# Gate and up side by side in weight chunks, 256-column low-rank products, a turned front, and variance sums, banks and copies moved

## The reference

```python
def _dequant(codes, scales):              # blocks of 64
    w = NF4[codes]
    return (w.reshape(O, I // 64, 64) * scales[:, :, None]).reshape(O, I)
def _lin_lora(x, W, A, B):
    return x @ W.T + (x @ A.T) @ B.T      # A: 16 x I, B: O x 16
q, k, v = (_lin_lora(x, W[i], A[i], B[i]) for i in range(3))
x1 = x + _lin_lora((q + k + v) / 3, Wo, Ao, Bo)
h  = silu(_lin_lora(x1, Wg, Ag, Bg)) * _lin_lora(x1, Wu, Au, Bu)     # 1792 wide
x  = layernorm(x + x1 + _lin_lora(h, Wd, Ad, Bd))
x  = layernorm(x + _lin_lora(x, Wf, Af, Bf))   # NF4, rank 64, factor 1/4
x  = layernorm(x + attention(x))               # one head of 128 per batch
x  = layernorm(x + experts(x))                 # 64 experts of rank 16, best 16
```

## Time and profile before

| what | us |
| --- | --- |
| time, median of 3 runs (lowest, highest) | 526.01 (523.20, 526.26) |
| the profiled execution | 525.68 |
| its span in the trace | 523.9 |
| TensorE busy | 486.5 |
| VectorE, ScalarE, GpSimd busy | 374.4, 291.4, 284.2 |

### The profile page before, as it was taken

One profiled execution on the slowest core, in us unless ns is written; L12 is line 12 of the kernel. 1 busy time (PEld: TensorE's weight loads), 2 busy tenths in 40 slices (PEclk: granted clock), 3 DMA queues, 4 the chain that ended last, 5 costly groups with the idle time before them and its releaser, 6 DMA issues.

```text
span 523.9 us, 7456 instructions
## 1 busy us (share of the span) xinstructions
PE 486.5 (93%) x2248; PEld 393.9 (75%) x2248; DVE 374.4 (71%) x701; ACT 291.4 (56%) x539; POOL 284.2 (54%) x261
## 2 busy tenths in 40 slices
PE   2489899899999999999999998998998899999996
PEld 1246678688888888888888886887886788888884
DVE  5979889638897887997979953864368866366433
ACT  6979868555755675766666722625487422333021
POOL 4787756667555765765666755687479310110001
PEclk9999999899999999999999999998999999999998
DMA  7674523414223343442433203530000000000011
GB/s 199 226 238 145 137 73 103 143 40 119 78 85 101 100 112 91 109 119 80 120 99 101 60 0 114 192 128 1 1 0 1 1 1 22 20 21 21 1 41 40
DMA packets 21415, 43.01 MB, mean 82 GB/s; under 512 B 3328, under 2 KB 3456, under 8 KB 21120
## 3 DMA queue, kind: packets, MB, share of 16 engines
q1 hardware_dynamic: 21152, 42.16, 26.6%
q0 software_dynamic: 224, 0.38, 0.3%
HBM read 40.42 MB, written 2.10 MB: 81 GB/s over the span
## 4 chain that ended last, share of the span: by engine, by line
PE 70%; DVE 4%; issue 3%; ACT 2%; POOL 1%; ACTq 0%; DVEq 0%; POOLq 0%
PE bank L1114 63%; PE bank L1278 3%; PE bank L1127 2%; PE bank L1396 1%; ACT prob L1070 1%; PE bank L1136 1%; DVE bn L1601 1%; DVE rmax L1647 0%; ACT pT_hi L887 0%; DVE pT_lo L1453 0%; PE bank L1308 0%; PE bank L1309 0%; ACT eb_hi L887 0%; POOL rstd L870 0%; DVE xs L1449 0%
## 5 line engine op out<-in xcount | busy, mean ns | idle before, releaser
L789 POOL TENSOR_TENSOR wf<-value,scale 128x512 f32<-128x512 f32 x50 | 64.6, 1291 | 72.7 <-DVE value L1485 68.9
L1114 PE MATMUL bank<-x_hi,gu_hi 128*128 128x512 f32 x224 | 89.1, 398 | 0.0
L1114 PE MATMUL bank<-x_lo,gu_hi 128*128 128x512 f32 x224 | 87.8, 392 | 0.0
L1114 PE MATMUL bank<-x_hi,gu_lo 128*128 128x512 f32 x224 | 87.7, 392 | 0.0
L870 POOL TENSOR_TENSOR rstd<-veps,neg_half 128x1 f32<-128x1 f32 x24 | 13.2, 551 | 106.5 <-issue 105.1
L895 ACT ACTIVATE bank<-code 128x512 f32<-128x512 int32 x124 | 68.6, 585 | 0.0
L1449 DVE TENSOR_TENSOR xs<-bank,xs 128x512 f32<-128x512 f32 x56 | 38.5, 688 | 26.2 <-PE bank L1114 25.8
L1463 DVE SCALAR_TENSOR_TENSOR low<-bent,bank 128x512 f32<-128x512 f32 x62 | 42.4, 683 | 14.7 <-ACT bank L895 6.4
L1114 PEld LDWEIGHTS bank<-x_hi,gu_lo 128*128 128x128 f32 x224 | 42.3, 189 | 9.0
L1114 PEld LDWEIGHTS bank<-x_hi,gu_hi 128*128 128x128 f32 x224 | 42.6, 190 | 7.9
L1114 PEld LDWEIGHTS bank<-x_lo,gu_hi 128*128 128x128 f32 x224 | 42.4, 189 | 8.0
(11 more groups left out here) (225 smaller groups left out, 1174.4 us busy)
## 6 DMA issues: line engine op xcount, KB each, us to landing
code<-codes SPq DMA_DIRECT2D x62, 256.0 KB, 2.7
scale<-scales SPq DMA_DIRECT2D x100, 128.0 KB, 3.0
xs<-xT SPq DMA_DIRECT2D x2, 1024.0 KB, 6.3
ea_raw<-ex_A SPq DMA_DIRECT2D x1, 2048.0 KB, 9.9
eb_raw<-ex_B SPq DMA_DIRECT2D x1, 2048.0 KB, 8.7
out<-rows SPq DMA_DIRECT2D x8, 256.0 KB, 2.0
bgu_raw<-loB_gu SPq DMA_DIRECT2D x1, 896.0 KB, 5.6
wqkv_raw<-w_qkv SPq DMA_DIRECT2D x1, 768.0 KB, 4.4
```

The source lines that it names most:

```text
L789: pool.tensor_tensor(w, v, scale[:, i % RING_CODES, :], ALU.mult).then_inc(scaled_done, 1)
L1114: last = nc.tensor.matmul(ps, a, b, start=start and i == 0 and n == 0, stop=stop and i == len(terms) - 1 and n == 2)
```

## The change

Chunks g and u now each hold half of the inputs, of gate and of up side by side: chunk ("g", f) has input blocks 0 and 1 for both, ("u", f) blocks 2 and 3. A low-rank product is two matmuls of 256 columns; its B matrix is loaded and split in five parts of three rounds instead of in two cuts. A unit takes six matmuls from one chunk and six from the other, with a wait ahead of each half. The order of the chunks in a round is u, d, g (of the round after) instead of g, u, d.

In the front, "out" of a chunk now stands behind "mid" of the next, mid's result lies in two buffers in SBUF instead of one bank of PSUM, a fourth code buffer is used, x is loaded in eight pieces, and the last three of the eight x splits stand behind the front. TensorE takes the sum products of q, k and v ahead of all three partials.

In the first rounds some ScalarE and VectorE steps change places. In the tail, down 5.7 goes to bank 6, batch 1's sums are made by VectorE behind its last x split, and the second mean stands behind ffn 2. SP's lora and x loads, semaphores and buffers are adapted.

```diff
+def beside_round(f):
+    chunks = [("u", f + 1), ("d", f + 1), ("g", f + 2)]
+    return [c for c in chunks if c[1] < NF]
...
+FRONT = 4 * KT
+RING_FRONT = 4
...
+LB_PART = 3
+XSPLIT_AFTER = [8, 10, 12, 13, 14]
+EXTRA_LOADS = {7: ["x0"], 8: ["x1"], 10: ["x2"], 11: ["x3"], 12: ["x4", "gate_a"], 13: ["gate_b0"], 14: ["x5"],
+               17: ["x6"], 18: ["x7", "down"]}
+PART_LOADS = {("d", 0): 1, ("g", 3): 2, ("u", 6): 3, ("u", 9): 4}
...
-    for j in range(4 * KT):
-        half(CHUNKS[j], 0)
-        if j == 3:
+    for j in range(FRONT):
+        order.append(("mid", CHUNKS[j]))
+        if 2 <= j < KT + 2:
+            order.append(("omerge", j - 2))
+        if j >= 9 and j % 3 == 0:
+            order.append(("acc", j // 3 - 3))
+        if j >= 11 and j % 3 == 2:
+            order.append(("m1", (j - 11) // 3))
+        if j:
+            order.append(("out", CHUNKS[j - 1]))
+        if j == 4:
             order.append(("eyes", 0))
-        half(CHUNKS[j], 1)
+        order += [("clip", CHUNKS[j]), ("low", CHUNKS[j + 1])]
+        if 2 <= j < KT + 2:
+            order.append(("osplit", j - 2))
         if j in XSPLIT_AFTER:
             order.append(("xsplit", XSPLIT_AFTER.index(j)))
-    due.clear()
+    order.append(("out", CHUNKS[FRONT - 1]))
...
+    order += [("mid", ("g", 0)), ("xsplit", 5), ("clip", ("g", 0)), ("low", ("u", 0)), ("m1", KT - 2), ("out", ("g", 0)),
+              ("mid", ("u", 0)), ("acc", KT - 1), ("clip", ("u", 0)), ("low", ("g", 1)), ("out", ("u", 0)), ("bprep", 0),
+              ("mid", ("g", 1)), ("clip", ("g", 1)), ("m1", KT - 1), ("bprep", 1), ("x1", 0), ("x1", 1), ("xsplit", 6)]
     alone(("g", 1), 1)
-    order += [("merge", ("g", 0)), ("x1", 2), ("split", ("g", 0)), ("dprep", 0), ("x1", 3), ("merge", ("u", 0))]
+    order += [("merge", ("g", 0)), ("x1", 2), ("split", ("g", 0)), ("xsplit", 7), ("dprep", 0), ("x1", 3),
+              ("merge", ("u", 0))]
...
-    order += [("hsplit", 0), ("silu", 1), ("merge", ("d", 0)), ("split", ("d", 0))]
-    alone(("u", 2), 1)
-    order.append(("h", 1))
+    order += [("hsplit", 0), ("merge", ("d", 0)), ("low", ("d", 2)), ("silu", 1), ("split", ("d", 0)), ("out", ("u", 2)),
+              ("h", 1), ("merge", ("d", 1))]
...
-    down:6.6 xa:1.1 fold:1.1 down:6.7 xa:1.2 xa:1.3 ffn:0 ffn:1 mean:0 fold:1.2 stat:1.0 stat:1.1 fold:1.3 norm:1.0 norm:1.1
-    ffn:2 stat:1.2 stat:1.3 norm:1.2 ffn:3 norm:1.3 ffn:4 mean:1 stat:1.4 turn:1.0 turn:1.1 norm:1.4 ffn:5 stat:1.5
+    down:6.6 xa:1.1 down:6.7 xa:1.2 xa:1.3 fold:1.1 fold:1.2 fold:1.3 ffn:0 ffn:1 mean:0 stat:1.0 stat:1.1 norm:1.0 norm:1.1
+    ffn:2 mean:1 stat:1.2 norm:1.2 ffn:3 stat:1.3 norm:1.3 ffn:4 turn:1.0 stat:1.4 turn:1.1 norm:1.4 ffn:5 stat:1.5
...
+        mid_front = at("mid_front", 130, [P, 2, 512])
...
+        def mid_at(j):
+            return mid_front[:, j % 2, :] if j < FRONT else mid_ps[:, :]
...
-            return bank[7] if gi < len(GROUPS) - 1 else bank[7 - n % 3]
+            if gi == len(GROUPS) - 1:
+                return bank[7 - n % 3]
+            return bank[6] if (gi, n) == (len(GROUPS) - 2, TT - 1) else bank[7]
...
+                    i = int(name[6:])
+                    if i:
+                        sp.wait_ge(bprep_done, i + 1)
+                    _, raw, cut = lb_part(i)
+                    sp.dma_start(raw, loB_gu[:, cut, :, :]).then_inc(bgu_in, 16)
...
+                    for h in range(2):
+                        m = 2 * "gu".index(kind) + h
+                        last = nc.tensor.matmul(lora_ps[:, 2 * h * P:2 * (h + 1) * P], la_gu[:, m * P:(m + 1) * P],
+                                                lb_gu[:, k // LB_PART % 2, k % LB_PART, :, :], start=True, stop=True)
...
+                for h in range(2):
+                    pe.wait_ge(hi_done, split_no(("gu"[h], f)))
+                    pe.wait_ge(lo_done, split_no(("gu"[h], f)))
+                    last = product(ps, [(gu_hi[:, s, k, g, :], gu_lo[:, s, k, g, :], x1_hi[:, k, tk], x1_lo[:, k, tk])
+                                        for k in (2 * h, 2 * h + 1)], start=h == 0, stop=h == 1)
...
+                if (gi, n) == (len(GROUPS) - 2, TT - 1):
+                    pe.wait_ge(h_done, 2 * NF - 1)
...
-                    nc.vector.scalar_tensor_tensor(mid_ps[:, :], code[:, j % RING_CODES, :], float(CODE_SHIFT),
-                                                   mid_ps[:, :], ALU.add, ALU.max).then_inc(mid_done, 1)
+                    nc.vector.scalar_tensor_tensor(mid_at(j), code_at(j), float(CODE_SHIFT), mid_at(j), ALU.add,
+                                                   ALU.max).then_inc(mid_done, 1)
...
+                elif kind == "fold" and item[1] == 1:
+                    o = item[2]
...
+                    nc.vector.tensor_tensor(x_sum[:, 1, :], xs[:, 1, 0, :] if o == 1 else x_sum[:, 1, :], xs[:, 1, o, :],
+                                            ALU.add).then_inc(folded[1], 1)
...
+                    nc.vector.tensor_tensor(square[:, 1, 0, :], square[:, 1, 0, :], square[:, 1, o, :], ALU.add)\
+                        .then_inc(folded[1], 1)
```

More of the change, by code:

```diff
@@ L218, in vector_order @@
     alone(("d", 1), 1)
-    order.append(("silu", 0))
+    order += [("silu", 0), ("bprep", 2)]
     alone(("g", 2))
@@ L222, in vector_order @@
     alone(("u", 2), 0)
-    order += [("hsplit", 0), ("silu", 1), ("merge", ("d", 0)), ("split", ("d", 0))]
-    alone(("u", 2), 1)
-    order.append(("h", 1))
+    order += [("hsplit", 0), ("merge", ("d", 0)), ("low", ("d", 2)), ("silu", 1), ("split", ("d", 0)), ("out", ("u", 2)),
+              ("h", 1), ("merge", ("d", 1))]
     alone(("d", 2), 0)
[L227 to L230, removed]
+    order += [("hsplit", 1), ("low", ("g", 3)), ("split", ("d", 1)), ("out", ("d", 2)), ("silu", 2)]
+    due += [[2, ("merge", ("d", 2))], [3, ("split", ("d", 2))]]
+    order += [("merge", ("g", 2)), ("split", ("g", 2))]
+    half(("g", 3), 0)
+    order += [("h", 2), ("merge", ("u", 2)), ("hsplit", 2), ("silu", 3)]
+    order.append(("split", ("u", 2)))
+    half(("g", 3), 1)
     unit_h(3)
@@ L233, in vector_order @@
         downs = downs_beside(f) + [None] * 4
-        ahead = [(m, f + 1) for m in "gud"] if f < NF - 1 else []
+        ahead = beside_round(f)
         ahead += [("f", FFN_AT[f])] if f in FFN_AT else []
@@ L273, in tensor_order @@
         downs = downs_beside(f) + [None] * 4
-        ahead = [(m, f + 1) for m in "gud"] if 1 <= f < NF - 1 else []
+        ahead = beside_round(f) if f else []
         late = ("f", FFN_AT[f]) if f in FFN_AT else None
@@ L278, in tensor_order @@
         elif f == 1:
-            beside = [*ahead[:2], None, None]
+            beside = [("g", 2), ahead[0], ahead[1], None]
         elif late:
-            beside = [ahead[0], ahead[1], ahead[2], None]
+            beside = [*ahead, None, None][:4]
         else:
@@ L555, in build @@
         square_done = sem("square_done")
-        folded = sem("folded")
+        folded = [sem(f"folded{b}") for b in range(NB)]
         mean_ready = sem("mean_ready")
@@ L609, in build, with code_slot, code_uses, code_before @@
         LAST = ("mix", TT - 1)
+        def code_slot(j):
+            return j % RING_FRONT if j < FRONT else (j - FRONT) % RING_CODES
+        def code_uses(j):
+            return sum(code_slot(m) == code_slot(j) for m in range(j + 1))
+        def code_before(j):
+            return max(m for m in range(j) if code_slot(m) == code_slot(j))
+        def code_at(j):
+            return code_fourth[:, :] if code_slot(j) == RING_CODES else code[:, code_slot(j), :]
+        def mid_at(j):
+            return mid_front[:, j % 2, :] if j < FRONT else mid_ps[:, :]
         def split_no(c):
@@ L703, in _, with load_code @@
         def _(sp):
[L705 to L716, removed]
+            def load_code(j):
+                sp.dma_start(code_at(j), codes[j]).then_inc(codes_in[code_slot(j)], 16)
@@ L723, in _ @@
                     sp.dma_start(lb_f[:, :], loB_f).then_inc(loraf_in, 16)
[L724 to L727, removed]
-                if c in SCALED:
[L729 to L736, removed]
+                sp.wait_ge(mid_done, code_before(j) + 1)
+                sp.wait_ge(top_ready, code_before(j) + 1)
+                load_code(j)
+                if j == RING_FRONT:
+                    load_scale(("o", KT - 1))
+                if c in SCALED:
+                    load_scale(c)
             sp.wait_ge(unit_ready, 2 * NF)
@@ L1176, in _ @@
                 if i:
-                    partial(i - 1, 1)
-                    partial(i - 1, 2)
+                    pe.wait_ge(m1hi_done, i)
+                    pe.wait_ge(m1lo_done, i)
+                    pe.wait_ge(xhi_done, i)
+                    pe.wait_ge(xlo_done, i)
+                    for r in range(KT - 1):
+                        partial(i - 1, r)
                 if i == 0:
```

193 lines of the change are left out of this document (110 added, 83 removed).

## The result

The changed kernel takes **530.63 us** (median of 4 runs, 529.7 to 531.43); the kernel before took 524.96 on the same chip. The ratio is 1.0108, with an interval of 1.007 to 1.0146: about 1% slower, where 518 had been forecast and 510 to 523 as the range. The profiled execution took 531.43 us, 5.75 more than that of before (525.68).

What follows compares the result with a forecast made beforehand. TensorE, busy 93% of the span, was taken to bound the kernel, with the front set by decoding codes. Front, x-split, merge, low-rank and tail terms summed to -7.7 us, giving about 518 us, range 510 to 523.

Steps and rivals of the forecast that it cites:

- chunk pairs and order: In the rounds: waits for second chunks, merges and lora loads stay hidden, some 4 us left over; cost zero.
- the term for the pairs: Sign for the rounds: if TensorE waits there, the zero cost given to chunk pairs is wrong.
- the merge of d0 and d1: Behind the front: the merge comes ahead of its reader, removing a TensorE wait and half clock, -2.2 and -1.9 us.
- The port: In the front: VectorE operations with two SBUF inputs take turns with GpSimd products, 7.4 us of delay.
- The front as a whole: Up to batch 0's last partial product: the turned front ends later, +1.6 us.
- The x splits: At batch 1's start: TensorE waits for GpSimd's split 7, +2.9 us, and the half clock follows, +1.9.
- Low-rank products: Two matmuls of 256 columns take 0.23 us instead of 0.40, 28 times: -0.7 and -4.1 us.
- The tail: Waits for down 5.7 (-2.0 us) and the second mean (-1.5) go, and the half clock (-1.7).
- The rivals: Port free 511 (0.20); no split delay 513 (0.10); longer port stops (0.07); late pairs 524.5 (0.06); columns alone 523 (0.04).
- the port at 539: Rival in the front: the port stops VectorE for longer, 539 us at the full 1.1 us each; chance 0.07.

Runs made afterwards that it cites:

- experiment 2: Changed kernel with x splits 6 and 7 moved up behind u0's mid, where GpSimd had been idle: 526.47 us.
- experiment 5: Changed kernel with round 12's decode order mended, x splits 6 and 7 early, and g2's merge ahead of g3's first operation: 517.26 us.
- experiment 8: Changed kernel with round 12, early x splits, g2's merge and PSUM mid repairs, plus down's load, last m1 and g0's merge reordered: 511.37 us.
- experiment 9: Kernel of experiment 8 with h of unit 2 and u2's merge moved ahead of g3's mid and clip: 509.65 us.
- experiment 3: Changed kernel with the front's mid back in the one PSUM bank: 526.28 us.
- experiment 4: Kernel before the change with only the front's mid placed in SBUF, one buffer, all waits as they were: 532.53 us.
- experiment 6: Changed kernel with round 12's decode order mended (520.4), gate and up low-rank products again four matmuls of 128 columns: 524.25 us.
- experiment 7: Changed kernel with round 12's decode order mended (520.4), tail undone (bank 7, batch 1 sums on GpSimd, old order): 527.44 us.

## Why the prediction was wrong, point by point

**The step that failed** is the one on chunk pairs and order: "Each stands one place earlier in the order, so I cost this at nothing", and at its end "All zero". I followed each chunk from its low-rank product to its *use* and found 4 us to spare. But the first reader of a merge is not the unit that uses the chunk: it is the *next low-rank product*, which needs the one bank that the merge empties. Between two of these there is one unit and one down, and what stands ahead of the merge in VectorE's order decides. My working has one round for all and nothing of round 12. That is the round that the turned order changes in kind: it keeps the ffn chunk, by which TensorE asks for its products earlier, but g13 has moved to the round before and no g14 takes its place, by which VectorE's order falls back to the slow beat. That cost 9.3 us in the trace, and taking it away gave 10.3 by the medians, 9.8 in the trace. With a zero there and the rest as measured, the kernel would have been at 520.4, within the range. Its nearness to 518 is partly luck: larger losses than forecast (the front, u2 and d2) stand beside a larger gain in the tail. The prediction's own sign ("if TensorE waits in the rounds, the term for the pairs is") pointed at the right term, though the second chunk of a pair held up nothing.

**The same reason, smaller, at the merge of d0 and d1.** The stall and its half clock went as forecast (4.21 for 4.1 and a product's 0.17). I named the merge of g2 as "next in line" and let two units cover it; they didn't, by 0.43, and the merge of u2 by 0.97: 1.95 in all by the ledger. In VectorE's order g3's "low" and d2's "out" stand ahead of the merge of g2, and each waited some 0.3 us for ScalarE; g3's mid, ahead of the merge of u2, waited 1.51. Experiments 2, 5 and 8 show that whatever TensorE gains ahead of this place is partly lost there until the order is mended (experiment 9).

**The port: right.** The 32 operations in SBUF took 7.0 us more than at 0.69 each (13.7, 11.1 and 4.3 us in the groups shown); I had 7.4. The Trainium skill (SBUF — State Buffer, section "SBUF: two separate sides") has the shared port held for a whole instruction, the other engine waiting; experiments 3 and 4 agree: v3's "out" 5.6 us earlier and 8.1 later. The front as a whole ended 1.5 later than I forecast in the profiled execution (69.40 for 67.9), by waits for ScalarE of 1.26, 0.33 and 0.33 in the first chunks, where I had left 0.7. Five other kernels with the same front ended it at 67.34 to 68.89, so this is about the spread of the front itself.

**The x splits: right.** 2.84 us of wait, which ends 0.1 after GpSimd's split 7; the half clock behind it cost 1.27, not the 1.9 I took from the earlier trace rows. GpSimd's split 7, and TensorE's timeline in the changed kernel, from the last partial of batch 0 on:

```profile
77.30 1.27 POOL L874 TENSOR_TENSOR x_lo<-xs,x_hi 128x512 fp32r<-128x512 f32 x1
```

```profile
69.40 0.47 PE L1188 MATMUL bank<-x_hi,m_hi 128*128 128x512 f32 x1 [1.46 <-ACT m_hi L1029]
...
78.67 0.77 PE L1188 MATMUL bank<-x_hi,m_hi 128*128 128x512 f32 x1 [2.84 <-issue]
...
80.08 0.63 PE L1188 MATMUL bank<-x_hi,m_hi 128*128 128x512 f32 x1
```

**Low-rank products: right in kind, too large.** Forecast 4.8, measured 3.5 in the trace of experiment 6 and 3.9 by the medians: from their first matmul to the next wide one, seven of the 28 pairs take 0.34 instead of 0.23. The formula for an isolated gap in the Trainium skill (TensorE: Matmul & The Clock Gate, section "Back-to-back issue gap") would have had no difference; the measurement decides, 0.39 against 0.23.

**The tail: right.** 6.1 in the ledger and 6.0 in experiment 7, for 5.2.

**The rivals.** None of them happened. The slower side that I had priced (the port at 539) was not the one that came.

What stays open: why some pairs take 0.34, what decides whether the half clock follows a wait of 1.5 to 2.6 us, and what makes the front end 2 us earlier or later from one execution to the next.

## What to carry to other kernels

When an order of work is turned by one, look for the place where it ends: a round with one item less can fall into another branch of a planner, and one such round cost 9.3 us, where all the rest of the change had gained 3.7. Follow each result to its *first* reader, and in an in-order queue ask what the operation ahead of it waits for: a merge whose inputs are there, placed behind an add that needs TensorE, makes TensorE wait for itself. Where operations of VectorE and GpSimd run side by side, keep one of the two VectorE operands in PSUM even if that costs a buffer: here the wait was 0.15 to 0.2 us per chunk, the port 0.44. And when gains of separate experiments are to be added, look in the traces for where each gain comes: 1.6 us of two of them stood in a place that a third edit mended.

## What the runs showed of the hardware

GpSimd pays for the shared port too: its products in the front grew from 1.04 to 1.45 and from 1.28 to 1.63 us.

The length of a wait did not tell by itself whether the half clock followed. Waits of 1.74 us (experiment 8) and of 2.46 us (experiment 3, ahead of the last partial of batch 0) were followed by matmuls at the full 2.4 GHz (granted 1.00 in each of the next four and three us). One of 1.85 us (experiment 2) was followed by 1.2 GHz (granted 0.50 from 108 to 111 us). And the wait of 2.58 us at u13 had 1.2 GHz behind it in the changed kernel and 2.4 GHz in experiments 2 and 3. Here is a stretch of 2 us behind it, first in the changed kernel and then in experiment 2 (columns as in the earlier trace rows):

```profile
298.00:300.00 2.00, 2.00 (x6) 1.57 (x5) 0.00 (x0) 0.00 (x0) 0.00 (x0) 0.50 0.00 0
...
294.00:296.00 2.00, 2.00 (x11) 1.68 (x11) 0.00 (x0) 0.00 (x0) 0.51 (x1) 1.00 0.03 8
```

Where a stall of this size is forecast, both ends belong into the range; here they are 1.6 us apart.
